# Last expert's final three tiles of the second layer by row blocks, and SyncE waiting for the last transfers

## The reference

```
x = x + xattn(layernorm(x), ctx, ctx, ...)     # 16 heads of 64, layer norm behind it
x = x + attn(layernorm(x), ...)                # 16 heads of 32, rotary positions
x = x + ffn(layernorm(x), W1, b1, W2, b2, Wr, br)

def ffn(x, ...):                               # xf: 1024 rows of 512
    logits = xf @ Wr + br                      # 8 experts
    masked = where(logits >= second largest, logits, -inf)
    weights = softmax(masked)
    h = gelu(xf @ W1[e] + b1[e])               # 512 -> 2048, for each expert e
    expert_out = h @ W2[e] + b2[e]             # 2048 -> 512
    out = sum over e of expert_out[e] * weights[:, e]
```

## Time and profile before

| what | value |
|---|---|
| median of 3 runs | 1742.57 us (1740.15 to 1744.72) |
| the profiled execution | 1737.34 us, its span 1735.5 us |
| mean granted clock of TensorE | 0.974 of full speed |
| TensorE busy | 1642.4 us, 95% of the span |
| VectorE, ScalarE, POOL busy | 51%, 40%, 18% |
| last product ends, as VectorE sees it | 1718.87 us |
| last output addition issued by POOL | 1722.75 us |
| end of the span | 1735.5 us |

### The profile page before, as it was taken

How to read it: one execution, slowest core, us unless ns; L and a number is a source line. 1 busy time by engine, 2 the same in 40 slices (tenths; PEclk the granted TensorE clock), 3 DMA queues, 4 the chain that set the end, 5 groups by cost and what they waited for, 6 DMA issues and landing times. The chain is left out here.

```text
span 1735.5 us, 26943 instructions
## 1 busy us (share of the span) xinstructions
PE 1642.4 (95%) x10858; PEld 1384.9 (80%) x10858; DVE 880.4 (51%) x1592; ACT 695.5 (40%) x1314; POOL 306.2 (18%) x257
## 2 busy tenths in 40 slices
PE   7999999999999999999999987994999999999886
PEld 6888888888888888888888766773888888888885
DVE  4344443443344434443443575785777457558842
ACT  5333333333333333333333433453655345345621
POOL 4201210011101110111010061465321011011101
PEclk9999999999999999999999998996899999999898
DMA  6601820111011101111002460113757337437711
GB/s 230 220 6 53 132 73 7 53 56 53 12 48 56 53 23 37 56 53 37 26 4 80 144 198 25 51 57 128 257 160 218 125 94 229 157 87 237 218 33 21
DMA packets 54070, 165.17 MB, mean 95 GB/s; under 512 B 10580, under 2 KB 10964, under 8 KB 53376
## 3 DMA queue, kind: packets, MB, share of 16 engines
q1 hardware_dynamic: 38032, 131.88, 22.3%
q0 software_dynamic: 15888, 31.19, 8.5%
HBM read 143.54 MB, written 55.64 MB: 115 GB/s over the span
## 5 line engine op out<-in xcount | busy, mean ns | idle before, releaser
L405 PE MATMUL psum<-ctx,Wk 128*128 128x512 f32 x1536 | 384.9, 399 | 0.0
L405 PE MATMUL psum<-Wv,ctx 128*128 128x512 f32 x1536 | 368.7, 389 | 0.0
L405 PEld LDWEIGHTS psum<-Wv,ctx 128*128 128x128 f32 x1536 | 288.3, 188 | 59.7
L405 PEld LDWEIGHTS psum<-ctx,Wk 128*128 128x128 f32 x1536 | 279.3, 188 | 55.4
L887 DVE SCALAR_TENSOR_TENSOR kT<-psum,bkc,kT 128x512 fp32r<-128x512 f32 x128 | 96.0, 750 | 387.9 <-ACT kT L1251 387.9
L405 PE MATMUL psum<-xgT,Wh 128*128 128x224 f32 (+5 forms) x1536 | 249.8, 316 | 13.4 <-issue 13.4
L405 PEld LDWEIGHTS psum<-xgT,Wh 128*128 128x128 f32 x1536 | 228.5, 196 | 30.6 <-issue 15.6
L746 PE MATMUL psum<-Wh,hs 128*128 128x512 f32 x1008 | 250.3, 394 | 0.5 <-DVE hs L1139 0.5
L746 PEld LDWEIGHTS psum<-Wh,hs 128*128 128x128 f32 x1008 | 185.1, 189 | 35.2 <-DVE hs L1139 0.9
L1251 ACT ACTIVATE kT<-psum,bkc 128x512 fp32r<-128x512 f32 x128 | 88.3, 690 | 247.6 <-PE psum L405 247.5
L1416 ACT ACTIVATE gl<-psum,b1c 128x512 f32<-128x512 f32 x128 | 87.7, 686 | 205.8 <-PE psum L405 205.7
(11 more groups left out here) (146 smaller groups left out, 1770.1 us busy)
## 6 DMA issues: line engine op xcount, KB each, us to landing
raw<-in_W SPq DMA_DIRECT2D x128, 512.0 KB, 3.8
expert_rows<-in_spare_rows SPq DMA_DIRECT2D x16, 1042.0 KB, 7.4
raw<-in_ctxT SPq DMA_DIRECT2D x32, 512.0 KB, 4.4
xg<-expert_rows POOLq DMA_DIRECT2D x32, 256.0 KB, 5.5
low_parts<-Olo POOLq DMA_DIRECT2D x32, 128.0 KB, 2.4
oT<-low_parts SPq DMA_DIRECT2D x8, 512.0 KB, 4.6
out_x<-x SPq DMA_DIRECT2D x12, 256.0 KB, 2.0
xs<-in_x SPq DMA_DIRECT2D x4, 512.0 KB, 6.6
```

Source lines behind the costliest of these rows:

```text
L405: mm = pe.matmul(dst, l, r, start=n == 0, stop=n == len(pairs) - 1)
```

## The change

1. TensorE, last expert only (q = E - 1). The `down` of tiles 13, 14 and 15 are no longer done tile by tile with all row blocks in each, but block by block with the three tiles in each (`last_downs`). The products are the same 27. `y_ready` is raised behind the last product of each block; the last block raises it by what is missing up to CH. `y_psum` of the last tile is raised by the sequencer, which waits for `y_ready` first.
2. VectorE, last expert: each block waits for `y_ready` of its own.
3. POOL, last expert: blocks that its width leaves out get a transfer of one row of 512 between two places of a scratch tensor, so that `out_wide` reaches the same count for each width (one such transfer here). Behind the last output addition POOL's `job` returns, with no wait for landings. The waits stand in the branch of the second round instead, which isn't entered here.
4. SyncE: waits for the landings of all output additions as the last thing that it does.

```
--- before.py
+++ after.py
@@ sync_program
+            sp.wait_ge(out_added, 32 * E)
+            sp.wait_ge(out_wide[E - 1], 32)
@@ tensor_program
+            def last_downs(q, width):
+
+                chunks = -(-width // P)
+                for c in range(chunks):
+                    for i in range(NI - LAG, NI):
+                        n = NI * q + i
+                        hr = hs[n % HS]
+                        if c == 0:
+                            pe.wait_ge(h_lo, n + 1)
+                        for m, (x, y) in enumerate(((0, 0), (0, 1), (1, 0))):
+                            mm = pe.matmul(bank[3 + c], hr[x][:, c * P:(c + 1) * P], Wh[i][y][:, 512:1024],
+                                           start=False, stop=i == NI - 1 and m == 2)
+                        if i == NI - 1:
+                            mm.then_inc(y_ready, 1 if c < chunks - 1 else CH - c)
+                        elif c == chunks - 1:
+                            mm.then_inc(y_psum, 1)
+                pe.wait_ge(y_ready, E - 1 + CH)
+                pe.sem_inc(y_psum, 1)
+
             def job(q, width, more):
                 for i in range(NI + LAG):
                     if i < NI:
                         up(q, i, width)
-                    if i >= LAG:
+                    if q == E - 1 and i == NI:
+                        last_downs(q, width)
+                    if i >= LAG and (i < NI or q != E - 1):
                         down(q, i - LAG, width)
@@ vector_program, weighted
-                    if c == 0:
-                        v.wait_ge(y_ready, q + 1)
+                    if q == E - 1:
+                        v.wait_ge(y_ready, q + c + 1)
+                    elif c == 0:
+                        v.wait_ge(y_ready, q + 1 if q < E else q + CH)
                     else:
                         v.wait_ge(y_psum, NI * (q + 1))
@@ gpsimd_program, job
                 g.wait_ge(meta_in[q % 2], 16 * (q // 2 + 1))
+                if q == E - 1:
+                    for c in range(width // P, CH):
+                        g.dma_start(residuals[0, c:c + 1], residuals[1, c:c + 1]).then_inc(out_wide[q], 16)
                 for c in range(width // P):
                     ...
+                if q == E - 1:
+                    return
                 g.wait_ge(out_added, 32 * (q + 1))
@@ gpsimd_program, second round
             with g.If(rows_of[E] > WIDE):
+                g.wait_ge(out_added, 32 * E)
+                g.wait_ge(out_wide[E - 1], 32)
+                g.wait_ge(y_done, CH * E)
+                g.sem_inc(scattered, 1)
                 fetch_rows(E)
```

## The result

| | before | after |
|---|---|---|
| median of 20 runs | 1745.24 us (1740.15 to 1753.09) | 1738.01 us (1730.76 to 1744.39) |
| ratio of after to before | | 0.9953, 95% interval 0.9940 to 0.9966 |
| span of the profiled execution | 1735.5 us | 1738.2 us |
| start of VectorE's block 2 | 1718.87 | 1727.70 |
| from there to the end of the span | 16.6 us | 10.5 us |

What follows compares the result with a forecast made beforehand. TensorE bounds the kernel, but the end is a series: products, VectorE, POOL's issues, landing, DRAIN. Gains of 2.37 and 4.10 make 6.47 us, from median 1742.57 to 1736.1 us, range 1732 to 1742.5.

Steps and rivals of the forecast that it cites:

- Row blocks: Last expert's products on TensorE: block 0 ready 2.76 us earlier, no stall at tile 15, 2.37 us gained.
- VectorE to GpSimd: From VectorE's end of each block to GpSimd's addition: 0.76 us, third addition issued from 1720.38 to 1721.94.
- The landing: Third output addition lands 5.3 us behind its issue, at 1725.7.
- GpSimd's DRAIN: End of GpSimd's program: DRAIN starts at 1722.25 without waiting for landings, takes 6.56 us; gain 4.10 us.
- The rival "between": GpSimd's DRAIN does part of its labour before the landing: time 1736.1 to 1739.6 us; chance 0.30, shared with DRAIN from landing.
- The rule on such records: Skill's rule for GpSimd's DRAIN: the record covers execution alone, not the wait ahead, so 6.56 us is work.
- TensorE's branches: TensorE's end, behind its new last wait: branches of 3.26 and 4.80 us, through at 1727.3, 1.5 ahead of GpSimd.
- The bound of twice 4.80: TensorE's end with both last branches at 4.80 us: through at 1728.9.
- The extra transfer: One more issue in GpSimd's idle time before the first addition, 0.77 us: costs nothing, at worst 0.8 us.
- SyncE: SyncE's wait for the landings ends at 1725.7, its DRAIN at about 1725.8, 3 us ahead of GpSimd.
- The slower rival: Entry of the last expert's code on TensorE: two more fetches and slow clock lose 11.9 us, 1748.0; chance 0.07.

Runs made afterwards that it cites:

- blocks_only: Changed kernel with GpSimd and SyncE as before, keeping the row blocks and TensorE's last wait; 0.9992 (0.9972 to 1.0012) of before, end 14.22 us behind the last product.
- late_pool: Changed kernel plus a 1.5 MB copy issued by GpSimd behind the last addition, SyncE waiting for it too; end 16.45 us behind the last product.
- no_adds: Changed kernel without the last expert's three output additions and without the extra transfer; end 8.75 us behind the last product.

## Why the prediction was right, and where its steps were off

The forecast, 6.5 us less, was right in sign and near in size: 6.1 us in the profiles, 8.2 (5.9 to 10.5) in the first timing, 6.5 (2.6 to 10.1) in the second. The profiles account for 6.1 to 6.3 us (16.65 and 16.78 against 10.52 and 10.56), which lies in both intervals; whether more than that is real was not settled. The mechanism of one step was wrong all the same: "The prediction is wrong if the DRAIN's length follows the landings", it said, and the length does. That the number came out near is luck in part, since other terms made up for it. Point by point:

- **Row blocks.** Right. Block 0 is taken at 1723.63, 4.07 ahead of block 2; foretold were 1718.87 - 1714.75 = 4.12. No stall at tile 15. `blocks_only` gave 2.43, the sum had 2.37.
- **VectorE to GpSimd.** The 0.76 of the earlier trace rows was put on all three blocks; it belongs to a wait that stands by itself, which is there before and in `blocks_only`, for the first addition alone. In after it is 0.28. So the third addition came at 1.07 rather than at 1.55: gain 2.85 in place of 2.37.
- **The landing.** 5.3 behind the issue was foretold, 5.55 it was, so at 6.62 for 6.87.
- **GpSimd's DRAIN.** This is the step that failed. "It is therefore not a wait for data in flight" was drawn from a DRAIN that had nothing left to wait for. It is a labour of 6.3 to 6.6 us with a wait in its middle. It began 2 us earlier than foretold (1.41, not 3.4, since its record starts while the issue still runs), took 8.82 in place of 6.56, and ended at 10.22 where the sum had 9.98. The change overlaps only the part ahead of the wait: 7.22 from landing to the DRAIN's end became 3.61, so 3.6 us, where the prediction put 4.1 on this step. Counted from the landing that was foretold, 6.87, the DRAIN would have ended at 10.48; the third addition, half a us earlier than foretold, took half of that error away. The rival "between", part of the labour done early, is what happened; its end was put between the forecast and 3.5 us later, and it came 0.2 later.
- **The rule on such records** (the Trainium skill, Perfetto Trace Analysis, section Sequencer-only Instruction) can't be used as I used it. The record covers what the instruction does, and here that includes waiting for landings: `late_pool` stretched it to 14.86. The measurement decides.
- **TensorE's branches.** The place was right, the size too small: foretold through at 1727.3, so 8.5 behind the last product, with 8.06 us for both branches. They took 9.95, and it was through at 10.27, not 1.5 us ahead of GpSimd's DRAIN but the last to arrive, by 0.1 us. `no_adds`, without the traffic, came out at 8.51. The bound of twice 4.80 was too low by 0.35: beside transfers one branch took 5.4, and 8.25 in `late_pool`.
- **The extra transfer.** Right: at 1667.4, in GpSimd's idle time, 0.58 us. That it would shorten the next wait was not seen.
- **SyncE.** Right: through 3.6 us before the end.
- **The slower rival.** It didn't happen. TensorE stood still for 5.53 us at the last expert's entry, 5.23 before. That entry is 8.4 us later in the profile of after, but 14.2 us later in the second profile of the kernel before, so a shift of this size needs no change to the kernel.

## What to carry to other kernels

In these runs the DRAIN at the end of GpSimd's program, behind transfers that it had issued, had a part that ran while they were in flight and a part that didn't, so have another engine wait for the landings and let GpSimd go on. What is left counts from the last landing, and the work is then to bring that landing forward (issue the earlier blocks sooner, cut the last one to its rows), until the DRAIN's own 6.6 us behind the last issue are the longer. Ahead of a sequencer's branch to far code (code that has to be fetched first) at the end of a program, put no wait that isn't needed: a branch that began 4.2 us ahead of the last product's end moved behind it, and TensorE was the last to arrive in one profile (by 0.1 us), 0.7 ahead in the other. And a price read where nothing is in flight is not the price beside traffic.

## What was not expected of the hardware

- GpSimd's DRAIN: 0.17 us before any transfer, 6.32 to 6.57 when all have landed, and, begun early, it ends 3.61 to 3.65 us behind the last landing of GpSimd's transfers in eight profiles, whether it starts 4.0 or 11.2 us before that landing. What it does in those microseconds no view shows. How it behaves if the landing comes sooner than 4.0 us behind its start was not tried.
- The first of TensorE's two branches to far code was longer with more traffic beside it: it took 3.26 to 3.7 us with none or little, 4.1 to 4.7 beside the additions, 6.9 beside SyncE's copy. The second took 4.75 with no additions at all, 4.7 to 5.9 with them, and 8.25 beside GpSimd's copy. The Trainium skill (Runtime: NRT & Kernel Launch, section Instruction fetch mechanics) says that such code has to be fetched by a transfer, and that fits.
- From VectorE's end to the start of GpSimd's addition 0.28 us passed in after, and 0.76 before and in `blocks_only`, where the wait has a row of its own.
